# The inverse deviation of the second normalisation as a power on GpSimd, in a convolution and mixture-of-experts block

## The reference

```
x = x + conv3x3(quant(ln_c(x)), quant(w))      # ln_c over the 64 channels, eps 1e-6; quant: blocks of 16
t = tokens(x)                                  # 8192 tokens of 64 channels
n = (t - mean(t)) / sqrt(var(t) + 1e-5)        # the second normalisation
p = softmax(n @ gate_w + gate_b); the two largest of 8 are kept as gates
t = t + sum_e gate_e * (gelu(n @ W1[e] + b1[e]) @ W2[e] + b2[e])
```

## Time and profile before

| | |
|---|---|
| median of three runs | 216.85 us (216.72 to 216.9) |
| profiled execution | 217.73 us, its span 215.8 us |
| PE busy | 183.6 us, 85% of the span |
| DVE busy | 146.8 us, 68% |
| POOL busy | 124.9 us, 58% |
| ACT busy | 116.6 us, 54% |
| mean granted clock of PE | 0.945 of 2.4 GHz |

### The profile page before, as it was taken

How to read it: one execution, slowest core, us unless ns; L and a number is a source line. 1 busy time by engine, 2 the same in 40 slices (tenths; PEclk the granted TensorE clock), 3 DMA queues, 4 the chain that set the end, 5 groups by cost and what they waited for, 6 DMA issues and landing times.

```text
span 215.8 us, 3603 instructions
## 1 busy us (share of the span) xinstructions
PE 183.6 (85%) x958; PEld 71.8 (33%) x958; DVE 146.8 (68%) x459; ACT 116.6 (54%) x153; POOL 124.9 (58%) x117
## 2 busy tenths in 40 slices
PE   2966297877756397989999999999999999999990
PEld 2954134434556243422222222222222222222220
DVE  0899999999977996387484584684683683344352
ACT  2439713170078474449665665665666656656640
POOL 7697225767253251346766576566567557666763
PEclk9999859699978769999999999999999999999997
DMA  6940000000000038658479479299298198397101
GB/s 187 308 70 3 0 2 2 2 0 0 3 0 0 0 102 169 134 122 181 96 162 205 96 171 205 60 199 211 72 206 181 65 206 172 87 198 162 52 0 49
DMA packets 16316, 22.33 MB, mean 103 GB/s; under 512 B 2344, under 2 KB 8112, under 8 KB 16304
## 3 DMA queue, kind: packets, MB, share of 16 engines
q1 hardware_dynamic: 16144, 22.04, 45.4%
q10 hardware_dynamic: 160, 0.15, 0.2%
HBM read 19.82 MB, written 2.36 MB: 103 GB/s over the span
## 4 chain that ended last, share of the span: by engine, by line
PE 51%; DVE 27%; DMA 9%; issue 6%; ACT 3%; SPq 1%; DVEq 1%; POOLq 1%; POOL 1%; ACTq 0%
PE ps L1093 26%; PE ps L1078 24%; DMA gbc<-gate_rows 6%; DVE ssum L615 3%; DVE xn L702 3%; DVE xn L721 3%; DVE xn L627 3%; DMA cw<-in_conv_w 2%; DVE w_lo L675 2%; DVE y_sb L854 1%; DVE gbc L698 1%; ACT hl L490 1%; DVE topi L815 1%; DVE work L727 1%; ACT work L419 1%
## 5 line engine op out<-in xcount | busy, mean ns | idle before, releaser
L400 POOL TENSOR_TENSOR x<-x,y_sb 128x512 f32 (+1 forms) x63 | 80.1, 1271 | 52.2 <-DVE y_sb L854 51.4
L543 ACT ACTIVATE work<-ps,bias_sb,w_back 128x1024 f32<-128x1024 f32 x64 | 76.9, 1204 | 49.7 <-PE ps L1078 49.6
L854 DVE SCALAR_TENSOR_TENSOR y_sb<-ps,bias_sb,gbc 128x512 f32<-128x512 f32 x64 | 47.9, 750 | 53.2 <-PE ps L1093 42.9
L1093 PE MATMUL ps<-work,w_sb 128*64 128x512 f32 x256 | 68.8, 617 | 1.2 <-DVE y_sb L854 1.1
L1078 PE MATMUL ps<-xT,w_hi 128*128 (+1 forms) x128 | 39.6, 392 | 0.0
L1078 PE MATMUL ps<-xT,w_lo 128*128 (+1 forms) x128 | 39.0, 387 | 0.0
L993 PE MATMUL ps<-qpad,cw_bd 128*128 128x512 bf16 x72 | 21.6, 457 | 6.3 <-POOL qpad L355 6.3
L1093 PEld LDWEIGHTS ps<-work,w_sb 128*64 128x64 f32 x256 | 12.8, 135 | 29.0 <-issue 24.2
L1078 PEld LDWEIGHTS ps<-xT,w_hi 128*128 128x128 f16 x128 | 8.3, 100 | 41.7 <-issue 40.6
L355 POOL TENSOR_TENSOR qpad<-work,xn 128x512 bf16<-128x512 f32 (+1 forms) x8 | 10.5, 1310 | 15.9 <-DVE work L727 15.9
L379 POOL TENSOR_TENSOR hl<-xn,hl x8 | 9.2, 1155 | 15.9 <-DVE hl L777 9.0
(11 more groups left out here) (112 smaller groups left out, 182.7 us busy)
## 6 DMA issues: line engine op xcount, KB each, us to landing
gbc<-gate_rows SPq DMA_DIRECT2D x16, 768.0 KB, 10.6
gbc<-gate_rows SPq DMA_DIRECT2D x16, 256.0 KB, 3.9
x_sb<-in_x SPq DMA_DIRECT2D x8, 256.0 KB, 5.0
out<-x SPq DMA_DIRECT2D x8, 256.0 KB, 10.9
w_raw<-in_W SPq DMA_DIRECT2D x2, 256.0 KB, 5.8
w_sb<-in_W SPq DMA_DIRECT2D x1, 256.0 KB
gate_rows<-gateT SPq DMA_DIRECT2D x8, 32.0 KB, 2.0
cw<-in_conv_w ACTq DMA_DIRECT2D x2, 72.0 KB, 4.0
```

The lines of the kernel that those rows point to most:

```text
L400: pool.tensor_tensor(x2[:, ds(c * W, W)], x2[:, ds(c * W, W)], y_sb[:, u % H_RING, :], ALU.add).then_inc(added, 1)
L543: act.activation(h_sb[:, u % H_RING, :], bank(H + 2 * (u % 2), 2 * W), ACT.Gelu, bias=b1_sb[:, u:u + 1], scale=w_back[:, u:u + 1]).then_in ...
L854: dve.scalar_tensor_tensor(y_sb[:, u % H_RING, :], bank(Y + u % 2), b2_sb[:, u:u + 1], gbc[:, slot, u, :], ALU.add, ALU.mult).then_inc(wei ...
L1093: last = pe.matmul(ps[r * CH:(r + 1) * CH, (Y + u % 2) * W:(Y + u % 2 + 1) * W], w2_sb[:, u, :], h_sb[:, u % H_RING, r * W:(r + 1) * W], s ...
```

## The change

The deviation and its reciprocal of the second normalisation are replaced by two POOL operations per part: a tensor_scalar (ssum/64 + eps into std) and a tensor_tensor with the operation pow against a tile filled with -0.5. The constant tile eps2 goes, the tile power comes, filled by a linked memset at the start. On POOL parts 0 and 1 stand ahead of low_half(0), part 2 stands between low_half(3) and low_half(4), and the two hardware loops of low halves are written out, with waits on constants. The first normalisation keeps its square root and reciprocal.

```diff
-        eps2 = sb("eps2", [128, 1])
+        power = sb("power", [128, 4 * GROUPS])
@@ POOL
-            pool.memset(eps1[:, :], LN1_EPS)
-            pool.memset(eps2[:, :], LN2_EPS).then_inc(eps_ready, 1)
+            pool.memset(eps1[:, :], LN1_EPS).then_inc(eps_ready, 1)
+            link(pool.memset(power[:, :], -0.5))
...
-            with pool.Fori(0, EARLY) as c:
-
-                wait_alone(pool, (xh_ready, c + 1))
+            def inverse_deviations(k):
+
+                first, last = LN2_PARTS[k]
+                n = (last - first) * GROUPS
+                pool.wait_ge(ss2, last)
+                flat = lambda t: t[:, first:last, :].rearrange("p z g -> p (z g)")
+                link(pool.tensor_scalar(flat(std), flat(ssum), 1.0 / CH, LN2_EPS, ALU.mult, ALU.add))
+                pool.tensor_tensor(flat(rstd), flat(std), power[:, 0:n], ALU.pow).then_inc(rstd2, 1)
+
+            inverse_deviations(0)
+            inverse_deviations(1)
+            low_half_after = lambda c: (pool.wait_ge(xh_ready, c + 1) if c < EARLY
+                                        else pool.wait_ge(xh_by_dve, c + 1 - EARLY))
+            for c in range(EARLY):
+                low_half_after(c)
                 low_half(c)
-            with pool.Fori(EARLY, NCH) as c:
-
-                wait_alone(pool, (xh_by_dve, c + 1 - EARLY))
+            inverse_deviations(2)
+            for c in range(EARLY, NCH):
+                low_half_after(c)
                 low_half(c)
@@ ACT
-            deviations(LN2_PARTS[0], ss2, eps2, std2)
...
-            deviations(LN2_PARTS[1], ss2, eps2, std2)
...
-            deviations(LN2_PARTS[2], ss2, eps2, std2)
@@ DVE
-            invert(LN2_PARTS, 0, std2, rstd2)
...
-            invert(LN2_PARTS, 1, std2, rstd2)
...
-            invert(LN2_PARTS, 2, std2, rstd2)
```

More of the change, by code:

```diff
@@ L196, in program @@
         ss2 = sem("ss2")
-        std2 = sem("std2")
+        var2 = sem("var2")
         rstd2 = sem("rstd2")
```

## The result

The changed kernel takes 225.04 us (median of four runs, 223.79 to 225.56) against 216.83 before (a fourth run has moved the median from 216.85): 1.037 times as long, 95% interval 1.033 to 1.042, or +8.2 us. The direction was forecast; the size, +1.8 with a range to 223.2, was not. The profiled execution took 225.56 us with a span of 223.7.

What follows compares the result with a forecast made beforehand. Bound: the chain through the second normalisation and routing to chunk 0's gates, 53 to 74 us. +1.25 (parts 0 and 1) + 0.55 (part 2) = +1.8 us on 216.85 gives 218.6; own range 217.4 to 219.4, overall 216.9 to 223.2.

Steps and rivals of the forecast that it cites:

- What bounds the kernel: 53 to 74 us, second normalisation to gates of chunk 0: a microsecond before those gates is one of the time.
- What goes, at most 0.64 us: Three square roots on ScalarE cost nothing; three reciprocals removed from VectorE win at most 0.27 + 0.27 + 0.1 us.
- The price of the power: GpSimd power taken as ten plain operations, 21 ns a column: 0.52 us for 16 columns, 0.86 for 32.
- my ceiling of forty: Upper price of a GpSimd power, forty plain operations, 85 ns a column: 1.54 us for 16 columns, 2.9 for 32.
- Case A: Rival: power far dearer, at the ceiling price; L794 4.3 us late, 223.2 us in all; chance 0.2.
- The estimate from the Trainium skill: Ten dependent steps at 4 cycles per element, 33 ns a column: power 0.7 and 1.25 us, sum about +2.8 us.
- Part 0, in time but paid through the port: Chunks 0 and 1: result in time up to 1.6 us, but GpSimd's port block holds VectorE's L675: +0.5 us.
- Part 1, the wait in front of low_half(0): Chunks 2 and 3: low_half(0) queues behind the power, transposes 2.8 us late; +1.25 us together with part 0's 0.5.
- Part 2, "the result is covered": Chunks 4 to 7: power ready before xn(4), but L799 held +0.65 us, reciprocal gives 0.1 back: +0.55 us.
- Rival D: Faster: TensorE's clock stays at 2.4 GHz through 62 to 68 us, saved reciprocals reach the end; 216.45 us; chance 0.13.

Runs made afterwards that it cites:

- experiment 3: Changed kernel with a product in place of the power, plus 24 filler transposes on TensorE before the transposes of chunk 0: 216.33 us, 0.9967 of before.
- experiment 2: Changed kernel with the power replaced by a product in the same instruction form, queue order and waits kept: 218.11 us, 1.0053 of before.
- part 0 alone: Kernel before with only chunks 0 and 1 by the power on GpSimd, the rest by square root and reciprocal, low halves written out: 216.73 us, 0.9990.
- Experiments 3 and 6: The second of these: changed kernel, real power kept, with 46 filler transposes on TensorE before the transposes of chunk 0: 223.05 us, 1.027 of before.
- Measured alone: Only chunks 4 to 7 by the power on GpSimd, the other chunks by square root and reciprocal as before: 220.69 us, 1.0189.
- experiment 8: Changed kernel with chunks 4 to 7 powered one by one in GpSimd's gaps, chunks 2 and 3 back to square root and reciprocal: 217.37 us, 1.0015.
- experiment 9: Kernel before with only the two low-half loops written out with waits on constants, and the unused power tile's memset: 216.81 us, 0.9990.

## Why the prediction was right or wrong

- **What bounds the kernel: right.** The stretch from 53 to 74 us is on the chain, and 7.9 of the 8.6 us lost before the gates of chunk 0 reached the end; the wait for the gate rows, shorter by 0.93 us, covers the rest.
- **What goes, at most 0.64 us: the size fits, but isn't shown by itself.** With the price removed and the clock held the kernel was 0.33% faster (experiment 3); 0.33 us of that is seen at the gates of chunk 0, and the share of the clock in the rest isn't separated.
- **The price of the power: wrong, and this is the step that failed.** "A power needs a logarithm and an exponential; I take it as ten plain operations, 21 ns a column." It is 159 ns, 7.6 times that and nearly twice my ceiling of forty (85 ns). Of the +8.2, about 7 is this price (experiment 2). Nothing in the trace of before bounded it from above; forty was a count I made up, and the range should not have ended there. Case A named this outcome with a chance of 0.2 and a time of 223.2, still too low. Its transposes at 66.4 met the measured 66.19 by luck: 1.4 us too little for the second power, and 1.5 of a hold in part 0 that did not happen. Its "L794 4.3 late" does not follow from its own steps either: with transposes at 66.4, the steps of part 1 give about 3.4.
- **The estimate from the Trainium skill was nearer than mine and not near:** 33 ns a column from the Trainium skill (GPSIMD Engine Reference, 7. Performance pitfalls for Q7 kernels) by ten dependent steps. It too rested on my ten. By the steps of the prediction it would have made the sum +2.6, not +2.8.
- **Part 0, in time but paid through the port: first half right, second wrong.** It was in time although the power took more than the 1.6 us I allowed: I had counted to the last L675 at 57.0, but the reader is xn(0) at 58.6, so the room was 3 us, and 2.93 just fitted. I forecast +0.5 from L675 being held; L684 kept its length and part 0 alone measured no change. I had carried the lock from 512 plain columns to 16 of a power. The same wrong hold stood in part 2 at L799. Its two gifts to my sum (+0.76 in part 0, +0.65 in part 2) made the forecast look nearer than it was: without them it was about 217.25.
- **Part 1, the wait in front of low_half(0): right mechanism.** My steps gave transposes of 0 at 64.3 and L794 at 69.7. With the measured price and without the hold of part 0 (sum of chunk 3 at 61.78, not 62.25) the same steps start the transposes at 66.2, as observed. The clock was mis-sized: I let 2.4 GHz return during the centring of 6, and it stayed at 1.2 through both. Experiments 3 and 6 price that at 1.8 and 2.0 us.
- **Part 2, "the result is covered": wrong through the price.** Between L794 (68.44) and xn(4) (70.21) lay 1.8 us; 0.86 us would have fitted, 5.43 stuck out by 3.85. Measured alone: +3.7.
- **Rival D, faster if the clock stays up: its condition was real.** Cheap price with the clock held gave 216.33, its 216.45. The nearness is in part luck: the price in that run was 0.22 us and not the 0.5 of rival D, and against the kernel before timed beside it (216.95) it gained 0.6 us, not 0.4. The change itself meets neither condition.

## What to carry to other kernels

Price an operation that the trace doesn't hold by measuring it, or leave the upper end open: a function on GpSimd cost 75 plain operations a column here, and no neighbour's row said so. A slow instruction is harmless where its result has slack and nothing behind it in its queue is awaited, so before moving work to an in-order engine look at what queues up behind the new wait; here two low halves did, and TensorE, idle for them, came back at half clock. When the same work must stay, cutting it into pieces that fit the gaps removed all but some tenths of a microsecond of the loss of its part (experiment 8).

## What the hardware showed that I had not expected

- A GpSimd power computes for 5.43 us (32 columns) without holding VectorE's two-input instructions (at most 0.32 us, median 0.29), while a plain 512-wide product of 1.26 us holds one for 1.25.
- Useless transposes on TensorE, 24 in 3.8 us of idleness, made the kernel of experiment 2 1.8 us faster by keeping it at 2.4 GHz; centrings went from 1.82 to 0.97 us.
- In a GpSimd loop with its count and addresses in registers the low half began 0.34 us after its input was there, written out with constants under 0.1 (experiment 9). It was worth nothing here.
